# Two bias sums on GpSimd in other steps, and a prefetch hint on a loop's branch back

## The chip, the cores and the metric

The kernel runs on one core of one Trainium2 chip. The metric is the device time of the whole kernel in microseconds (us). Inputs and the weights lie in HBM. Engines are named as in the profile: PE is TensorE (PEld its weight loads), DVE is VectorE, ACT is ScalarE, POOL is GpSimd, SP is SyncE, which here only issues DMAs.

## The reference

One transformer layer on x of 16 batches x 1024 positions x 256 features, in float32: layer norm, causal attention with 16 heads of 16 features and rotary positions, beside it a feed-forward part whose output goes through a spiking neuron of five time steps, and a residual sum.

```python
xn = _layernorm(x)
x = x + attn(xn, Wq, bq, Wk, bk, Wv, bv, Wo, bo) + ffn(xn, W_fc, W_proj)

# attn
Q, K, V = (split_heads(xn @ W.T + b) for ...); Q, K = _rope(Q), _rope(K)
scores = where(causal, einsum('bhqd,bhkd->bhqk', Q, K) * 0.25, -1e9)
out = softmax(scores) @ V ; out = concat(out) @ Wo.T + bo

# ffn
h = square(relu(xn @ W_fc.T)); y = h @ W_proj.T
mem = 0.9 * mem + y - (mem > 1); spk = mem > 1      # five steps
ffn = sum(spk) / 5
```

## The kernel before

**Intervals and steps.** All five engines run programs written out by hand, tied by semaphores. A program is a row of intervals b = -1 to 15. Interval b does the attention of batch b and, beside it, the projections and the feed-forward part of batch b + 1, the layer norm of b + 2, and the output of batch b - 1. Intervals -1, 0, 14 and 15 are written out; b = 1 to 13 are one loop on each engine (`Fori(1, B - 2)`), whose closing instruction is a compare-and-branch: L1238 on PE, L683 on ACT, L960 on DVE, L589 on POOL, L485 on SP. It jumps back twelve times and falls through once. Each interval has 18 steps (n = 0 to 17), and in every step each engine does the parts that the tables at the head of the file give to that step, in the order in which its `interval` function names them. No scheduler moves anything.

**Attention.** 36 units per batch, two per step: `scores` on PE (L1156, tile pair), exp on ACT (L643, tile probs), for units on the diagonal `mask` on POOL (L556: one affine_select per 128 columns, one or two per unit), and the weighing of V by probs on PE (L1173), a step or more later by the table RUN_AT. Unit 14 stands in step 7, and its weighing in step 8. PE waits there for the mask (`mask_done`). The sums for 512 queries of four heads go out by `take_numer` on DVE (L882).

**Feed-forward.** Sixteen blocks i, by the tables EXPAND and CONTRACT: `expand` on PE (L986), relu on ACT (L634), square and high part on DVE (L846, L848), low part h_lo on POOL (L548), `contract` on PE (L1137), which waits for h_lo. Products are split in high and low parts so that three matmuls stand for one exact one. The result y is counted against thresholds on DVE (L859, L862), and the count is added to rs (L867).

**The sums of x and bias.** rs[0] and rs[1] hold 256 rows of x each, loaded by SP (L363). `add_bias` on POOL (L531 to L534) waits for the load and adds bo_sb, in two instructions of 128 x 256 (L533) per buffer, so four for both. It is called twice per batch: for the second half of the rows of batch b in step BIAS_HERE_AT, and for the first half of batch b + 1 in step BIAS_NEXT_AT. The reader is DVE's L867 (waits `rs_biased`); for the first half of b + 1 it stands in step 15, for the second half of b in step 9. SP issues the loads of the first kind in step 0 and those of the second in step 12.

**Rotary part.** Four groups u of queries and keys: PE projects (L986), DVE rotates into rot and rot_b (L769 to L776), POOL adds the two (`sum_qk`, L538, in step 3 + u), ACT squares the sum and rounds it to planes (L615, L618), DVE takes the low part (L780), SP stores both to HBM (qk_dram), and for u = 2 and 3 DVE may write rot_b only when the store of u - 2 has landed (L775).

Of the kernel before, what the change touches and what calls it, by code (L numbers as in the profile page):

```python
# [10 lines left out]
B, S, D = 16, 1024, 256  # L11
# [106 lines left out]
SPIKES_NEXT = {14 + 2 * a + part: (a, part) for a in range(2) for part in range(2)}  # L118
BIAS_HERE_AT, BIAS_NEXT_AT = 7, 14
STATS_AT = {10: range(0, 4), 11: range(4, 8)}  # L120
# [27 lines left out]
def layer_kernel(nc, x, wqk, bqk, wv, bv, wfc, wproj, wo, bo, tables, consts, selectors, out):  # L148
    edges = spike_thresholds()
    with ExitStack() as ctx:  # L150
# [157 lines left out]
        def _(sp):  # L308
# [175 lines left out]
            interval(0, True, False, True, True)  # L484
            with sp.Fori(1, B - 2) as b:  # L485
                interval(b, True, True, True, True)
# [16 lines left out]
        def _(pool):  # L503
# [26 lines left out]
            def add_bias(b, g, a):  # L530
                pool.wait_ge(rs_in[a], (b * 2 + g + 1) * 16)  # L531
                for t in range(2):
                    ins = pool.tensor_tensor(rs[a][:, t, :], rs[a][:, t, :], bo_sb[:, :], ALU.add)  # L533
                ins.then_inc(rs_biased, 1)  # L534
# [24 lines left out]
            def interval(b, att, last, more, norm, first=False):  # L559
                nb = b + 1  # L560
                for n in range(NSTEP):
                    if more and n in SUM_QK_AT:
                        sum_qk(nb, SUM_QK_AT[n])
                    if att and n == BIAS_HERE_AT:
                        for a in range(2):
                            add_bias(b, 1, a)
                    if norm and n == ROOT_AT:
# [9 lines left out]
                    if more and n in EXPAND_LATE:  # L577
                        h_low(nb, EXPAND_LATE[n])
                    if more and n == BIAS_NEXT_AT:
                        if first:  # L580
                            pool.wait_ge(bias_done, 1)
                        for a in range(2):
                            add_bias(nb, 0, a)
# [4 lines left out]
            interval(0, True, False, True, True)  # L588
            with pool.Fori(1, B - 2) as b:  # L589
                interval(b, True, True, True, True)  # L590
# [13 lines left out]
        def _(act):  # L604
# [77 lines left out]
            interval(0, True, False, True, True)  # L682
            with act.Fori(1, B - 2) as b:  # L683
                interval(b, True, True, True, True)
# [11 lines left out]
        def _(dve):  # L696
# [262 lines left out]
            interval(0, True, False, True, True)  # L959
            with dve.Fori(1, B - 2) as b:  # L960
                interval(b, True, True, True, True)
# [20 lines left out]
        def _(pe):  # L982
# [254 lines left out]
            interval(0, True, False, True, True)  # L1237
            with pe.Fori(1, B - 2) as b:  # L1238
                interval(b, True, True, True, True)
# [67 lines left out]
```

## Time and profile before

| | us |
|---|---|
| median of 3 runs | 2351.49 |
| lowest, highest | 2349.76, 2353.95 |
| the profiled execution | 2352.46 |
| its span in the trace | 2348.6 |
| PE busy | 2184.8 (93%) |
| DVE, ACT, POOL busy | 1444.0, 1435.0, 1114.9 (61%, 61%, 47%) |
| granted TensorE clock, mean | 0.976 |

The profile is of one execution. Matmuls are pipelined and their ends are modelled, so a busy PE is not one at its peak; "issue" is time in which an engine waited for nothing that the profile shows, instruction fetch among it. A wait for several semaphores is put down to the one that came last. In the timelines each row is start, duration, engine, line, operation, tiles and shapes, count, and in brackets the idle time of the engine before it, with what ended it. [...]

### The profile page before, as it was taken

To read this page: it belongs to the slowest core of one execution; us is meant where nothing else is said; L and a number is where in the kernel's file an instruction comes from. 1 tells how busy PE (TensorE), PEld (TensorE's weight loads), DVE (VectorE), ACT (ScalarE), POOL (GpSimd) and SP (SyncE) were. 2 spreads that over 40 slices of the span, in tenths; PEclk is the share of its full clock that TensorE was granted. 3 is DMA by queue.
4 is the path that set the end of the run, shared out by engine and by line. 5 is a ranking of instruction groups with operands and counts; after the bars stand their busy time and mean duration, and the time that the engine had idled before them with its cause. 6 is when DMAs were issued, how large, how long until landed. Compare 5 with 4: busy or idle time off the path is not lost.

```text
span 2348.6 us, 48369 instructions
## 1 busy us (share of the span) xinstructions
PE 2184.8 (93%) x16260; PEld 1406.9 (60%) x16260; DVE 1444.0 (61%) x2108; ACT 1435.0 (61%) x1669; POOL 1114.9 (47%) x1065
## 2 busy tenths in 40 slices
PE   3799999999999999999999999999999999999985
PEld 2656656566665656666565666656666665666632
DVE  5646575665657666665765657567565766666431
ACT  2175766657566575666667566565666657566662
POOL 2445454553545545354553545546354554545420
PEclk8999999999999999999999999999999999999987
DMA  3243453635445263453535445263443536345342
GB/s 130 96 127 102 128 165 82 185 97 141 134 111 173 80 188 95 115 174 84 172 94 158 118 110 178 80 195 96 129 147 93 175 86 177 106 124 156 93 118 57
DMA packets 167725, 297.45 MB, mean 127 GB/s; under 512 B 25008, under 2 KB 112816, under 8 KB 155056
## 3 DMA queue, kind: packets, MB, share of 16 engines
q1 hardware_dynamic: 167472, 294.01, 43.6%
q8 instruction: 167, 2.74, 0.5%
q14 instruction: 86, 0.70, 0.1%
HBM read 173.32 MB, written 102.76 MB: 118 GB/s over the span
## 4 chain that ended last, share of the span: by engine, by line
PE 75%; issue 6%; DVE 6%; ACT 6%; POOL 5%; DMA 1%; SPq 0%; DVEq 0%; ACTq 0%; POOLq 0%
PE pair L986 28%; PE pair L1173 19%; PE pair L1137 14%; PE pair L1156 13%; ACT probs L643 4%; POOL rs L533 2%; POOL probs L556 2%; DVE count L862 1%; PE pair L998 1%; DVE stats L725 1%; ACT h_sq L634 1%; POOL rot L538 1%; DMA qk_dram<-rot_b 1%; DVE h_sq L846 1%; ACT squares L615 1%
## 5 line engine op out<-in xcount | busy, mean ns | idle before, releaser
L643 ACT ACTIVATE probs<-pair 128x1024 f32<-128x1024 f32 x1152 | 1116.7, 1026 | 579.5 <-PE pair L1156 579.0
L556 POOL TENSOR_SCALAR_AFFINE_SELECT probs<-probs 128x512 f32<-128x512 f32 x512 | 403.0, 806 | 534.4 <-ACT probs L643 534.4
L1173 PE MATMUL pair<-probs,v_sb 128*17 128x512 f32 (+3 forms) x6144 | 572.0, 505 | 50.7 <-POOL probs L556 39.1
L548 POOL TENSOR_TENSOR h_lo<-h_sq,h_hi 128x512 fp32r<-128x512 f32 x256 | 386.2, 1508 | 418.0 <-DVE h_hi L848 417.6
L1156 PE MATMUL pair<-q_ring,k_ring 64*128 64x512 f32 (+3 forms) x3072 | 444.0, 382 | 40.6 <-ACT probs L643 20.2
L1156 PEld LDWEIGHTS pair<-q_ring,k_ring 64*128 64x128 f32 x3072 | 228.0, 185 | 309.0 <-ACT probs L643 164.1
L846 DVE TENSOR_TENSOR h_sq<-h_sq 128x512 f32<-128x512 f32 x256 | 189.3, 740 | 352.6 <-ACT h_sq L634 350.9
L1173 PEld LDWEIGHTS pair<-probs,v_sb 128*17 128x17 f32 x6144 | 154.7, 99 | 357.8 <-issue 268.8
L1137 PE MATMUL pair<-wproj_hi,h_hi 128*128 128x256 f32 x1024 | 293.1, 286 | 5.1 <-POOL h_lo L548 5.0
L862 DVE SCALAR_TENSOR_TENSOR count<-y_sb,count 128x512 bf16<-128x512 f32 x256 | 291.7, 1140 | 6.7
L1137 PE MATMUL pair<-wproj_lo,h_hi 128*128 128x256 f32 x1024 | 290.0, 283 | 0.0
L1137 PE MATMUL pair<-wproj_hi,h_lo 128*128 128x256 f32 x1024 | 289.8, 283 | 0.0
L634 ACT ACTIVATE h_sq<-pair 128x512 f32<-128x512 f32 x256 | 153.5, 600 | 214.1 <-PE pair L986 214.1
L538 POOL TENSOR_TENSOR rot<-rot,rot_b 128x1024 f32<-128x1024 f32 x64 | 169.2, 2644 | 217.2 <-DVE rot_b L776 217.2
L986 PE MATMUL pair<-xT_hi,wfc_hi 128*128 128x512 f32 x512 | 222.5, 435 | 5.8 <-ACT h_sq L634 3.7
L1137 PEld LDWEIGHTS pair<-wproj_hi,h_hi 128*128 128x128 f32 x1024 | 195.8, 191 | 23.8 <-issue 11.0
L986 PE MATMUL pair<-xT_hi,wfc_lo 128*128 128x512 f32 x512 | 203.0, 396 | 0.0
L986 PE MATMUL pair<-xT_lo,wfc_hi 128*128 128x512 f32 x512 | 201.1, 393 | 0.0
L1137 PEld LDWEIGHTS pair<-wproj_lo,h_hi 128*128 128x128 f32 x1024 | 196.1, 192 | 5.6
L1137 PEld LDWEIGHTS pair<-wproj_hi,h_lo 128*128 128x128 f32 x1024 | 196.2, 192 | 0.0
L882 DVE COPY numer<-pair 128x512 f32<-128x512 f32 x128 | 87.6, 685 | 120.2 <-PE pair L1173 118.6
L780 DVE TENSOR_TENSOR rot_b<-rot,planes 128x1024 fp32r<-128x1024 f32 x64 | 148.5, 2321 | 1.9 <-ACT planes L618 1.9
(87 smaller groups left out, 2598.7 us busy)
## 6 DMA issues: line engine op xcount, KB each, us to landing
q_ring<-qk_dram SPq DMA_DIRECT2D x384, 128.0 KB
k_ring<-qk_dram SPq DMA_DIRECT2D x384, 128.0 KB
qk_dram<-planes SPq DMA_DIRECT2D x64, 512.0 KB, 2.8
qk_dram<-rot_b SPq DMA_DIRECT2D x64, 512.0 KB, 3.9
xn<-in_x SPq DMA_DIRECT2D x16, 1024.0 KB, 7.1
rs<-in_x SPq DMA_DIRECT2D x64, 256.0 KB, 2.8
acc_dram<-rs SPq DMA_DIRECT2D x64, 256.0 KB, 4.4
attn<-numer SPq DMA_DIRECT2D x256, 64.0 KB, 2.3
```

What stands on the lines that cost most here:

```text
L538: pool.tensor_tensor(rot[u % 2][:, :, :], rot[u % 2][:, :, :], rot_b[u % 2][:, :, :], ALU.add).then_inc(rot_sum, 1)
L548: pool.tensor_tensor(h_lo[i % HB][:, :], h_sq[i % HB][:, :], h_hi[i % HB][:, :].bitcast(F32), ALU.subtract).then_inc(h_lo_done, 1)
L556: ins = pool.affine_select(view, view, [[0, 4], [1, P]], ALU.is_ge, 0.0, base=0, channel_multiplier=-1)
L634: act.activation(h_sq[i % HB][:, :], fc_bank, ACT.Relu).then_inc(relu_done, 1)
L643: act.activation(probs[BUFFER[n]][:, 2 * pr:2 * pr + 2, :], pair[m % NSLOT][:, :, :], ACT.Exp, scale=SCALE).then_inc(exp_done, 1)
L780: dve.tensor_tensor(rot_b[u % 2][:, :, :].bitcast(F32R), rot[u % 2][:, :, :], planes[u % 2][:, :, :].bitcast(F32), ALU.subtract).then_inc( ...
L846: dve.tensor_tensor(sq, sq, sq, ALU.mult).then_inc(sq_h, 1)
L862: dve.scalar_tensor_tensor(count[:, :], y, edges[s], count[:, :], ALU.is_gt, ALU.add).then_inc(spike_step, 1)
L986: ins = pe.matmul(bank, lhsT, rhs, start=n == 0, stop=n == len(parts) - 1)
L1137: ins = pe.matmul(proj_bank[half][:, a * D:(a + 1) * D], h[:, cols], w[:, f, :], start=f == 0 and n == 0 and a == 0, stop=f == NFT - 1 and ...
L1156: ins = pe.matmul(pair[m % NSLOT][:, half, to:to + width(kt, g)], k_ring[rows, slot, pr, kt * P:(kt + 1) * P], q_ring[rows, slot, pr, q0:( ...
L1173: ins = pe.matmul(pv_bank[32 * i:32 * i + VW, q0 - g * G:G], v_sb[:, kt, 4 * quad + i, :], probs[BUFFER[n]][:, i, at:at + width(kt, g)], s ...
```

## The change

The tables that give the steps of the two calls of `add_bias` change from 7 and 14 to 2 and 13. In POOL's `interval` the first call moves from its place ahead of the masks of its step to one behind the masks and h_lo of the step. [...]

```diff
-BIAS_HERE_AT, BIAS_NEXT_AT = 7, 14
+BIAS_HERE_AT, BIAS_NEXT_AT = 2, 13
...
-                    if att and n == BIAS_HERE_AT:
-                        for a in range(2):
-                            add_bias(b, 1, a)
                     if norm and n == ROOT_AT:
                         root(nb + 1)
...
                     if more and n in EXPAND_LATE:
                         h_low(nb, EXPAND_LATE[n])
+                    if att and n == BIAS_HERE_AT:
+                        for a in range(2):
+                            add_bias(b, 1, a)
                     if more and n == BIAS_NEXT_AT:
...
-            with pool.Fori(1, B - 2) as b:
+            with nc.Fori(1, B - 2, engines=bass.OrderedEngineSet([pool.engine]), hint_back_edge=True) as b:
                 interval(b, True, True, True, True)
```

The last edit stands in the same form for sp, act, dve and pe.

POOL's queue in interval 0, steps 0 to 9 (L556 masks, L533 the sums, L538 rotary sums, L548 h_lo), before:

```order
41 L556 AFFINE_SELECT probs<-probs 128x4x128 x8
42 L538 TENSOR_TENSOR rot<-rot,rot_b 128x1024 x2
43 L556 AFFINE_SELECT probs<-probs 128x4x128
44 L538 TENSOR_TENSOR rot<-rot,rot_b 128x1024
45 L556 AFFINE_SELECT probs<-probs 128x4x128 x4
46 L538 TENSOR_TENSOR rot<-rot,rot_b 128x1024
47 L556 AFFINE_SELECT probs<-probs 128x4x128
48 L548 TENSOR_TENSOR h_lo_57<-h_sq_49,h_hi_53 128x512
49 L533 TENSOR_TENSOR rs<-rs,bo_sb 128x256 x4
50 L556 AFFINE_SELECT probs<-probs 128x4x128 x2
51 L548 TENSOR_TENSOR h_lo_58<-h_sq_50,h_hi_54 128x512
```

and now:

```order
41 L556 AFFINE_SELECT probs<-probs 128x4x128 x8
42 L533 TENSOR_TENSOR rs<-rs,bo_sb 128x256 x4
43 L538 TENSOR_TENSOR rot<-rot,rot_b 128x1024 x2
44 L556 AFFINE_SELECT probs<-probs 128x4x128
45 L538 TENSOR_TENSOR rot<-rot,rot_b 128x1024
46 L556 AFFINE_SELECT probs<-probs 128x4x128 x4
47 L538 TENSOR_TENSOR rot<-rot,rot_b 128x1024
48 L556 AFFINE_SELECT probs<-probs 128x4x128
49 L548 TENSOR_TENSOR h_lo_57<-h_sq_49,h_hi_53 128x512
50 L556 AFFINE_SELECT probs<-probs 128x4x128 x2
51 L548 TENSOR_TENSOR h_lo_58<-h_sq_50,h_hi_54 128x512
```

The four sums stood between the first h_lo and the two mask pieces of unit 14; they stand now between the masks of step 2 and the rotary sum of u = 0.

POOL's queue in interval 0, steps 13 and 14 (with the numbers of the buffers), before:

```order
83 L548 TENSOR_TENSOR h_lo2_59<-h_sq2_51,h_hi2_55 128x512
84 L556 AFFINE_SELECT probs1<-probs1 128x4x128 x2
85 L556 AFFINE_SELECT probs2<-probs2 128x4x128 x2
86 L548 TENSOR_TENSOR h_lo3_60<-h_sq3_52,h_hi3_56 128x512
87 L548 TENSOR_TENSOR h_lo0_57<-h_sq0_49,h_hi0_53 128x512
88 L533 TENSOR_TENSOR rs0<-rs0,bo_sb 128x256 x2
89 L533 TENSOR_TENSOR rs1<-rs1,bo_sb 128x256 x2
```

and now:

```order
83 L548 TENSOR_TENSOR h_lo2_59<-h_sq2_51,h_hi2_55 128x512
84 L533 TENSOR_TENSOR rs0<-rs0,bo_sb 128x256 x2
85 L533 TENSOR_TENSOR rs1<-rs1,bo_sb 128x256 x2
86 L556 AFFINE_SELECT probs1<-probs1 128x4x128 x2
87 L556 AFFINE_SELECT probs2<-probs2 128x4x128 x2
88 L548 TENSOR_TENSOR h_lo3_60<-h_sq3_52,h_hi3_56 128x512
89 L548 TENSOR_TENSOR h_lo0_57<-h_sq0_49,h_hi0_53 128x512
```

The four sums stand now ahead of the four mask pieces of step 14 (units 28 and 29) and two h_lo, which stood ahead of them.

PE's queue at the head of the loop:

```order
 L1137 MATMUL pair<-wproj_hi,h_lo_60 128x256
 L1238 UNCONDITIONAL_BRANCH
+L1238 BRANCH_PREFETCH_HINT
 L1238 ISA
 L1151 ISA
```

One instruction came in as the first of the loop's body; nothing else on PE moved. The other engines have the same at their loop's head.

## Rows read from the trace of the kernel before

**Rows 1.** The page: busy us by engine; chain that ended last.

```profile
PE 2184.8 (93%) x16260; PEld 1406.9 (60%) x16260; DVE 1444.0 (61%) x2108; ACT 1435.0 (61%) x1669; POOL 1114.9 (47%) x1065
...
PE 75%; issue 6%; DVE 6%; ACT 6%; POOL 5%; DMA 1%; SPq 0%; DVEq 0%; ACTq 0%; POOLq 0%
PE pair L986 28%; PE pair L1173 19%; PE pair L1137 14%; PE pair L1156 13%; ACT probs L643 4%; POOL rs L533 2%; POOL probs L556 2%; DVE count L862 1%; PE pair L998 1%; DVE stats L725 1%; ACT h_sq L634 1%; POOL rot L538 1%; DMA qk_dram<-rot_b 1%; DVE h_sq L846 1%; ACT squares L615 1%
```

**Rows 2.** Waits of PE: us in total, times, longest us.

```profile
PE pair L1173 <- POOL probs L556: 39.1, 18, 2.6
...
PE pair L1156 <- issue: 18.9, 12, 1.9
...
PE pair L1173 <- issue: 4.5, 9, 0.7
```

**Rows 3.** Closing branches: count, ns min/median/max, first and last start us.

```profile
L1238 PEldq COMPARE_BRANCH  x13: 83/3404/3830, 392.4 to 2071.5; - x13
...
L960 DVEq COMPARE_BRANCH  x13: 50/56/72, 394.7 to 2073.9; - x13
```

**Rows 4.** Timeline of PE at a taken edge: start us, us, operation, [idle before].

```profile
1095.60 0.73 PE L1156 MATMUL pair<-q_ring,k_ring 64*128 64x512 f32 x4 [1.39 <-issue]
...
1098.72 0.63 PE L1173 MATMUL pair<-probs,v_sb 128*17 128x256 f32 x8 [0.55 <-issue]
```

**Rows 5.** Timeline of PE where the loop falls through.

```profile
2074.34 2.34 PE L1173 MATMUL pair<-probs,v_sb 128*17 128x512 f32 x24
```

**Rows 6.** Timeline of all engines in step 7 of the interval from 1094.

```profile
1148.22 1.95 ACT L643 ACTIVATE probs<-pair 128x1024 f32<-128x1024 f32 x2
...
1149.62 2.17 POOL L548 TENSOR_TENSOR h_lo<-h_sq,h_hi 128x512 fp32r<-128x512 f32 x1 [2.40 <-DVE h_hi L848]
...
1151.75 2.80 POOL L533 TENSOR_TENSOR rs<-rs,bo_sb 128x256 f32<-128x256 f32 x4
...
1154.51 1.91 POOL L556 TENSOR_SCALAR_AFFINE_SELECT probs<-probs 128x512 f32<-128x512 f32 x2
...
1156.47 3.48 PE L1173 MATMUL pair<-probs,v_sb 128*17 128x384 f32 x24 [2.51 <-POOL probs L556]
```

**Rows 7.** Windows (before DMA share: the granted clock), then the timeline of PE.

```profile
1156.30:1159.70 3.40, 3.23 (x24) 0.83 (x24) 2.73 (x3) 0.00 (x0) 1.52 (x2) 0.50 1.00 303
...
1437.30:1440.70 3.40, 3.37 (x32) 1.61 (x33) 2.60 (x3) 0.98 (x2) 1.40 (x1) 1.00 1.00 303
...
737.81 1.92 PE L1173 MATMUL pair<-probs,v_sb 128*17 128x384 f32 x24 [2.54 <-POOL probs L556]
```

**Rows 8.** Timeline of step 2 and 3, POOL and ACT.

```profile
704.09 2.38 POOL L538 TENSOR_TENSOR rot<-rot,rot_b 128x1024 f32<-128x1024 f32 x1 [2.34 <-DVE rot_b L776]
...
1114.75 1.23 POOL L556 TENSOR_SCALAR_AFFINE_SELECT probs<-probs 128x512 f32<-128x512 f32 x2 [1.31 <-ACT probs L643]
...
1118.52 3.31 POOL L538 TENSOR_TENSOR rot<-rot,rot_b 128x1024 f32<-128x1024 f32 x1 [2.54 <-DVE rot_b L776]
...
1121.86 1.06 ACT L615 ACTIVATE squares<-rot 128x1024 bf16<-128x1024 f32 x1 [0.41 <-POOL rot L538]
```

**Rows 9.** The sums by line: count, ns min/median/max.

```profile
L533 POOL TENSOR_TENSOR rs<-rs,bo_sb x128: 714/734/1191, 108.5 to 2252.5; 128x256 f32<-128x256 f32 x128
```

**Rows 10.** Timeline of POOL in steps 13 and 14.

```profile
1203.27 2.19 POOL L548 TENSOR_TENSOR h_lo<-h_sq,h_hi 128x512 fp32r<-128x512 f32 x1 [1.09 <-DVE h_hi L848]
...
1209.64 1.68 POOL L556 TENSOR_SCALAR_AFFINE_SELECT probs<-probs 128x512 f32<-128x512 f32 x2 [1.36 <-ACT probs L643]
```

**Rows 11.** Timeline of PE in the first and in the last interval.

```profile
114.73 0.39 PE L1137 MATMUL pair<-wproj_hi,h_hi 128*128 128x256 f32 x1 [3.05 <-POOL h_lo L548]
...
2255.88 3.32 PE L1173 MATMUL pair<-probs,v_sb 128*17 128x384 f32 x24 [1.19 <-POOL probs L556]
```

**Rows 12.** Timeline of VectorE where it waits for a store, two intervals.

```profile
713.52 0.75 DVE L775 SCALAR_TENSOR_TENSOR rot_b<-pair,neg_bqk,table 128x512 f32<-128x512 f32 x1 [3.00 <-DMA qk_dram<-rot_b]
...
1132.08 0.75 DVE L775 SCALAR_TENSOR_TENSOR rot_b<-pair,neg_bqk,table 128x512 f32<-128x512 f32 x1 [1.48 <-DMA qk_dram<-rot_b]
```

More of the change, by code:

```diff
@@ L484, in _ @@
             interval(0, True, False, True, True)
-            with sp.Fori(1, B - 2) as b:
+            with nc.Fori(1, B - 2, engines=bass.OrderedEngineSet([sp.engine]), hint_back_edge=True) as b:
                 interval(b, True, True, True, True)
@@ L682, in _ @@
             interval(0, True, False, True, True)
-            with act.Fori(1, B - 2) as b:
+            with nc.Fori(1, B - 2, engines=bass.OrderedEngineSet([act.engine]), hint_back_edge=True) as b:
                 interval(b, True, True, True, True)
@@ L959, in _ @@
             interval(0, True, False, True, True)
-            with dve.Fori(1, B - 2) as b:
+            with nc.Fori(1, B - 2, engines=bass.OrderedEngineSet([dve.engine]), hint_back_edge=True) as b:
                 interval(b, True, True, True, True)
@@ L1237, in _ @@
             interval(0, True, False, True, True)
-            with pe.Fori(1, B - 2) as b:
+            with nc.Fori(1, B - 2, engines=bass.OrderedEngineSet([pe.engine]), hint_back_edge=True) as b:
                 interval(b, True, True, True, True)
```

## The prediction

> **What bounds the kernel now.** I read the page first: which engine is busy, and which holds the chain that ended last. TensorE (PE) is busy 93% of the span and holds 75% of the chain, while VectorE, ScalarE and GpSimd (POOL) are at 61%, 61% and 47%; so an idle moment elsewhere is worth something only where PE waits for it [rows 1]. The chain by line still has 2% for the bias sums (L533), which is about 44 us of a 2348.6 us span, and 6% of "issue" [rows 1]. Next I read the list of who waited for whom, for PE alone. Three entries matter: 39.1 us in 18 waits of the weighing matmuls (L1173) for masks on POOL, 18.9 us in 12 waits of the score matmuls (L1156) for "issue", and 4.5 us in 9 waits of L1173 for "issue" [rows 2]. Twelve is the number of times the loop branches back: it runs b = 1 to 13.
>
> A steady interval is (2073.9 - 394.7) / 12 = 139.93 us, from the first and last start of VectorE's closing branch [rows 3].
>
> **Part 1, the hint.** PE's closing branch took 83 ns in its shortest case and 3404 ns at the median; VectorE's took 50 to 72 ns [rows 3]. The 83 ns is the last pass, which falls through. So a taken branch costs PE's sequencer some 3.3 us. Its queue still holds matmuls, so the array stops for less: at 1095.60 it had stood for 1.39 us, and at 1098.72 again for 0.55 us, both "issue" [rows 4]. The fall-through gives a control, the same instructions without the jump: 24 matmuls of L1173 in 2.34 us without a break [rows 5], where after the taken branch the first 16 took 1.91 us and the other 8 came 0.55 us late [rows 4].
>
> The first stop sums to 18.9 us over the 12 edges. The second sums to 7.0: 4.5 us in 9 waits, and in the other three edges it is put down to a mask, inside the 39.1 us. That share follows from the rest of the entry: the 14 waits of b = 1 to 14 at about 2.53 us are 35.4, the one of b = 15 is 1.2, and 39.1 - 35.4 - 1.2 leaves 2.5 [rows 2, 6, 7, 11]. Together **25.9 us** (2.2 per edge). SP's own hint I cost at nothing, because what it issues first after the edge (the loads of rs) is read in step 2 at the earliest. The hint instruction itself has no row; the nearest, a short branch at 50 to 83 ns [rows 3], bounds it at 13 x 0.08 = 1 us on PE if nothing covered it, and PE's queue does.
>
> [...]
>
> **Part 2, the step-7 sums leave step 7.** In the interval from 1094 POOL ends an h_lo at 1151.79, does the four sums until 1154.55, then the two mask pieces of unit 14 until 1156.42, and PE starts at 1156.47 after 2.51 us idle [rows 6]. The scores behind that mask were weighed (exp) by 1150.17 [rows 6], so nothing but the sums stands before it. Without them the mask runs at 1151.8 and takes 1.3 (rows 8 show 1.23 for two pieces) to 1.9 us: done by 1153.1 to 1153.7. PE is free at 1156.47 - 2.51 = 1153.96. The whole wait goes, in b = 1 to 14: **35.4 us**. If both bounds went the other way, 0.5 us of each would stay.
>
> With the wait goes something else. [...] The 13 windows after this wait show 0.50 in nine of the intervals and 1.00 in four; one row of each kind stands in [rows 7]. What precedes each fall is the stop of PE. Without a stop I expect no fall: 9 x 1.56 = **14.0 us**. PE's idle time is nearly nil in the rest of the interval, so I take both as kept to its end.
>
> **Part 3, where the step-2 sums land.** They stand behind the masks of step 2 and ahead of the rotary sum of u = 0 (L538). POOL is idle for 2.54 us there, from 1115.98 to 1118.52 [rows 8]. A sum takes 734 ns at the median, 714 at least and 1191 at most [rows 9]: four are 2.9 us, 4.8 at worst. So L538 starts 0.4 us late (2.3 at worst). It took 3.31 us there and 2.38 for u = 1 [rows 8]; I estimate that what slows the first passes by while it waits. ScalarE waited 0.41 us for it [rows 8], so it is on the way to the stores of the planes, for which VectorE then waits 1.48 us, and in some intervals 3.00 [rows 12]. I charge 0.3 us x 14 = **+4 us**, bounds 0 and +2.3 x 14 = +32. Behind the sums in POOL's queue stand that L538 and the masks from step 4 on. The sums wait for a load of rs that SP issues in step 0, two steps ahead, and I cost that wait at nothing.
>
> **Part 4, from step 14 to 13.** POOL ends an h_lo at 1205.46, then has two pairs of masks, the second of which its exp allows only at 1209.64; it ends at 1211.32 [rows 10]. Four sums from 1205.46 end at 1208.4 (1210.2 at worst), the first pair by 1209.7, the second, still held by its exp, by 1211.4. That is where they end today, and PE does not wait for them today. Nothing on PE: 0. VectorE no longer waits for the sums in step 15, but has slack there. In the first interval there is no attention and this VectorE wait is on the path: PE stood 3.05 us for an h_lo at 114.73 [rows 11], which VectorE squares only after it has read the sums. I take **-3 us**, once.
>
> The last interval (b = 15) has one mask wait of 1.19 us with 24 matmuls at 3.32 us [rows 11]: 1.2 + 1.4 = 2.6 at most, of which ScalarE's chain takes some: **-2 us**.
>
> Sum against this execution: -25.9 - 35.4 - 14.0 + 4 - 3 - 2 = -76.3 us. The profiled run took 2352.46 us (span 2348.6), 0.97 above the median of the three runs, 2351.49. So about 2276.2 profiled, **2275.5 us** as a median: 3.2% faster. A steady interval should be 139.93 - 2.2 - 2.5 - 9/12 x 1.56 + 0.3 = 134.4 us.
>
> **Rivals.**
> A. *The hint does nothing on PE.* The branch still takes 3.3 us. [...] Time 2275.5 + 25.9 = 2301. Chance 0.12.
> B. *Second stop stays*: the head is there at once, the block after it is not. Worth 7.0 at most: 2282. By the times in [rows 4] PE has work to cover it. Chance 0.10, inside the range.
> C. *The step-2 sums push the rotary sum by 1 us or more*, and the stores of the planes with it, so that VectorE waits and PE behind it; or the long wait of 3.00 us [rows 12], today in few intervals, comes in most (13 x 1.5 = 20 us). 2285 to 2300. For it: the chain is tight, 0.41 us. Chance 0.15.
> D. *Slower than before.* [...] Chance 0.02.
>
> **How the numbers follow.** The forecast, with B, has 0.70: its own range is 2266 (no charge in part 3, and none of the longer waits of [rows 12] left) to 2285. C has 0.15, A 0.12, D 0.02, and 0.01 is left for no change. The range from 2266 to 2300 takes in the forecast and C and stops short of A. A measurement of this kernel can tell about 0.2% (5 us) from no change; all but D and the rest lie beyond that: faster 0.97, same 0.01, slower 0.02.
>
> **What would show it.** PE's closing branch near 0.1 us at its median, and no "issue" wait of L1156 twelve times. The waits of L1173 for POOL down from 39.1 us to under 5. A granted clock of 1.00 through steps 7 and 8 of every interval. Idle time of POOL ahead of the first L538 gone, and ScalarE's wait for it still under 1 us. Steady interval 134 to 135 us. Wrong would be: the branch still at 3.3 us (A), VectorE's wait for the store of rot_b above 2 us in most intervals (C), or new "issue" stops of PE in mid-interval (D).

## The result: 3.7% faster, 3 us below the forecast range

| | before | changed kernel |
|---|---|---|
| median, us | 2350.62 (6 runs, 2347.09 to 2353.95) | 2262.97 (6 runs, 2257.88 to 2268.82) |
| ratio | 1 | 0.9627, interval 0.9609 to 0.9645 |
| profiled execution, us | 2352.46 | 2264.27 |
| its span, us | 2348.6 | 2260.7 |
| granted TensorE clock, mean | 0.976 | 0.986 |
| PE busy, us | 2184.8 | 2158.7 |
| a steady interval, us | 139.93 | 133.69 |

The forecast was 2275.5 us with a range from 2266 to 2300. The change went the way that was forecast, and PE's two kinds of stops went as described, but the time ended 12.5 us below the forecast and 3 us below the range.

The page of the changed kernel, busy time by engine and the chain that ended last, answers to [rows 1]:

```profile
PE 2158.7 (95%) x16260; PEld 1402.0 (62%) x16260; DVE 1436.7 (64%) x2108; ACT 1434.9 (63%) x1669; POOL 1091.0 (48%) x1065
...
PE 82%; DVE 6%; ACT 4%; issue 4%; POOL 2%; DMA 1%; SPq 0%; DVEq 0%; ACTq 0%; POOLq 0%
```

"POOL rs L533" is gone from the chain by line, POOL's share has fallen from 5% to 2%, and PE's has risen from 75% to 82% of a span that is 88 us shorter. PE's own busy time fell by 26 us though it does the same 16260 matmuls: the mean granted clock rose from 0.976 to 0.986, so fewer of them ran at the lower level, 0.50.

The list of PE's waits (us in total, times, longest us) answers to [rows 2]. In the answer as a whole there is no "issue" wait of L1156 or L1173 any more, and of the mask waits one is left:

```profile
PE pair L1156 <- ACT probs L643: 20.8, 33, 1.7
...
PE pair L1173 <- POOL probs L556: 0.2, 1, 0.2
```

39.1 us in 18 waits have become 0.2 us in one, and 18.9 + 4.5 us of "issue" have become nothing. The closing branches (count, ns min/median/max, first and last start), which answer to [rows 3], show the first cause:

```profile
L1238 PEldq BRANCH_PREFETCH_HINT  x13: 36/36/55, 254.8 to 1858.8; - x13
...
L1238 PEldq COMPARE_BRANCH  x13: 88/357/399, 388.3 to 1992.5; - x13
...
L960 DVEq COMPARE_BRANCH  x13: 55/61/90, 390.6 to 1994.9; - x13
```

PE's taken branch went from 3404 to 357 ns at its median. The hint instruction itself takes 36 ns. A steady interval is (1994.9 - 390.6) / 12 = 133.69 us.

The timeline of PE at a taken edge (start, us, operation) answers to [rows 4]:

```profile
1057.62 0.28 PE L1137 MATMUL pair<-wproj_hi,h_lo 128*128 128x256 f32 x1
1057.83 0.73 PE L1156 MATMUL pair<-q_ring,k_ring 64*128 64x512 f32 x4
1058.49 2.34 PE L1173 MATMUL pair<-probs,v_sb 128*17 128x512 f32 x24
1060.77 0.79 PE L1156 MATMUL pair<-q_ring,k_ring 64*128 64x384 f32 x8
```

No row has a bracket: there was no idle time. The 24 matmuls of L1173 run in one piece, in the 2.34 us of the pass that falls through [rows 5]. Both stops of [rows 4] are gone.

The timeline of step 7 in an interval of the changed kernel, POOL and PE, answers to [rows 6]:

```profile
1111.08 2.17 POOL L548 TENSOR_TENSOR h_lo<-h_sq,h_hi 128x512 fp32r<-128x512 f32 x1 [2.22 <-DVE h_hi L848]
...
1113.21 1.22 POOL L556 TENSOR_SCALAR_AFFINE_SELECT probs<-probs 128x512 f32<-128x512 f32 x2
...
1115.35 1.92 PE L1173 MATMUL pair<-probs,v_sb 128*17 128x384 f32 x24
```

The mask follows the h_lo at once, takes 1.22 us instead of 1.91, and ends at 1114.43. PE begins on it at 1115.35 with no idle time, so the mask is there 0.92 us early. The matmuls take 1.92 us instead of 3.48, because the clock stays up. The window over this place (the number before the DMA share is the granted clock) answers to [rows 7]:

```profile
1114.00:1118.00 4.00, 4.00 (x37) 1.60 (x36) 3.80 (x11) 2.69 (x4) 1.72 (x2) 1.00 0.75 182
```

PE is busy without a gap at the upper level. From b = 2 to 13 the granted clock never falls to the lower level.

### The profile page after: what moved, and what is told of

Its sections match the earlier page's. It is cut to its first block, busy times and chain, and to the rows that moved or that the text cites. A ratio compares the mean times of both kernels' runs of the same rounds, so it can differ in the third digit from the quotient of the medians.

```text
span 2260.7 us, 48434 instructions
## 1 busy us (share of the span) xinstructions
PE 2158.7 (95%) x16260; PEld 1402.0 (62%) x16260; DVE 1436.7 (64%) x2108; ACT 1434.9 (63%) x1669; POOL 1091.0 (48%) x1065
## 4 chain that ended last, share of the span: by engine, by line
PE 82%; DVE 6%; ACT 4%; issue 4%; POOL 2%; DMA 1%; SPq 0%; DVEq 0%; ACTq 0%; POOLq 0%
PE pair L986 31%; PE pair L1173 20%; PE pair L1156 15%; PE pair L1137 15%; ACT probs L643 3%; DVE count L862 2%; PE pair L998 1%; DVE stats L725 1%; POOL rot L538 1%; PE pair L1070 1%; DMA qk_dram<-rot_b 1%; ACT h_sq L634 1%; POOL probs L556 1%; DVE h_sq L846 1%; DVE denom L785 1%
## 5 line engine op out<-in xcount | busy, mean ns | idle before, releaser
L556 POOL TENSOR_SCALAR_AFFINE_SELECT probs<-probs 128x512 f32<-128x512 f32 x512 | 376.7, 756 | 507.4 <-ACT probs L643 507.4
L548 POOL TENSOR_TENSOR h_lo<-h_sq,h_hi 128x512 fp32r<-128x512 f32 x256 | 385.8, 1507 | 427.6 <-DVE h_hi L848 427.1
L1173 PE MATMUL pair<-probs,v_sb 128*17 128x512 f32 (+3 forms) x6144 | 551.4, 492 | 4.4 <-DVE numer L882 3.4
L1156 PE MATMUL pair<-q_ring,k_ring 64*128 64x512 f32 (+3 forms) x3072 | 443.1, 382 | 22.2 <-ACT probs L643 20.8
L846 DVE TENSOR_TENSOR h_sq<-h_sq 128x512 f32<-128x512 f32 x256 | 202.8, 792 | 330.9 <-ACT h_sq L634 330.8
L1156 PEld LDWEIGHTS pair<-q_ring,k_ring 64*128 64x128 f32 x3072 | 227.3, 185 | 282.8 <-ACT probs L643 183.9
L1173 PEld LDWEIGHTS pair<-probs,v_sb 128*17 128x17 f32 x6144 | 152.6, 97 | 298.9 <-issue 263.9
L862 DVE SCALAR_TENSOR_TENSOR count<-y_sb,count 128x512 bf16<-128x512 f32 x256 | 296.8, 1159 | 6.7
L538 POOL TENSOR_TENSOR rot<-rot,rot_b 128x1024 f32<-128x1024 f32 x64 | 170.2, 2659 | 172.3 <-DVE rot_b L776 172.3
```

The source lines that it names most:

```text
L538: pool.tensor_tensor(rot[u % 2][:, :, :], rot[u % 2][:, :, :], rot_b[u % 2][:, :, :], ALU.add).then_inc(rot_sum, 1)
L548: pool.tensor_tensor(h_lo[i % HB][:, :], h_sq[i % HB][:, :], h_hi[i % HB][:, :].bitcast(F32), ALU.subtract).then_inc(h_lo_done, 1)
L556: ins = pool.affine_select(view, view, [[0, 4], [1, P]], ALU.is_ge, 0.0, base=0, channel_multiplier=-1)
L846: dve.tensor_tensor(sq, sq, sq, ALU.mult).then_inc(sq_h, 1)
L862: dve.scalar_tensor_tensor(count[:, :], y, edges[s], count[:, :], ALU.is_gt, ALU.add).then_inc(spike_step, 1)
L1156: ins = pe.matmul(pair[m % NSLOT][:, half, to:to + width(kt, g)], k_ring[rows, slot, pr, kt * P:(kt + 1) * P], q_ring[rows, slot, pr, q0:( ...
```

## Where the time went: an account by stretches

Every interval has the same instructions on VectorE, so the starts of the same instruction in two traces can be subtracted. I cut each of the intervals b = 2 to 13 at three instructions of VectorE, counted from its closing branch (L960): the rotation (L770) of group u = 2, which lies about a quarter of the way in; a square (L846) some 19 us further; and a square in step 8, behind the mask wait. The table has the mean of the twelve intervals in us. "Falls" are intervals in which the granted clock drops to 0.50 behind an edge or behind step 7.

| kernel | edge and steps 0 to 3 | to step 5 | steps 6 to 8 | the rest | interval | falls |
|---|---|---|---|---|---|---|
| before | 35.73 | 18.77 | 14.12 | 71.31 | 139.93 | 9, all behind step 7 |
| changed | 33.31 | 18.71 | 10.35 | 71.31 | 133.68 | 0 |

The first column is what a taken edge costs, 2.42 us. The third is the mask wait and the clock behind it: 3.77 us, of which 2.60 is in every interval (12.95 us without a fall against 10.35) and 1.17 is the mean of the falls. The second column holds VectorE's waits for the stores of rot_b. The fourth does not move in any kernel of this study. Each kernel's account is that of one execution, the profiled one. Together 6.25 us per interval, 75 us of the 87.9 by which the span fell. The rest is in the intervals at the ends, and comes below.

## The experiments

The theory at this point: the time is PE's, in two independent places, the edge (hint) and step 7 (mask, then clock); the move from step 14 to 13 and the hints of the other engines do nothing. The rivals: the hints of the other engines matter too, the gain of the sums comes from step 13, or the steps themselves matter and not the order behind the mask.

### One part alone

Only the hints (x1):

```diff
-            with pool.Fori(1, B - 2) as b:
+            with nc.Fori(1, B - 2, engines=bass.OrderedEngineSet([pool.engine]), hint_back_edge=True) as b:
```

and the same for the other four engines.

> The kernel before with the hint on all five loops and the sums left in steps 7 and 14. My theory: the edge alone is worth the two stops of PE, 2.2 us, plus some 0.26 us that the array lost in restarting (the aligned traces of before and after show 2.42 us per edge), so 12 x 2.42 = 29 us: about 2350.6 - 29 = 2322 us. PE still waits 2.5 us for the mask of unit 14 in b = 1 to 14, and the clock still falls after it. Rival 1 (the hint and the sums need each other: a PE that is earlier only waits longer for the mask): under 10 us of gain, the waits for the mask longer than 2.5 us. Rival 2 (the hint alone explains the excess over the forecast): over 38 us.

Measured: 2312.91 us, ratio 0.9833 (0.9814 to 0.9853) to a before of 2353.15. That is 40 us, more than the edges alone can give, 12 x 2.42 = 29, and 9 us below the 2322 that I had expected. The account shows 33.31, 18.68, 13.18, 71.32, interval 136.49. The first column is exactly that of the changed kernel. The third has come down by 0.94 us though the sums are still ahead of the mask: the falls went from nine to two. Two windows behind step 7 of this kernel, one of an interval with a fall and one without:

```profile
588.70:592.10 3.40, 2.79 (x24) 0.83 (x24) 3.16 (x4) 0.00 (x0) 1.96 (x2) 0.50 1.01 319
725.00:729.00 4.00, 2.26 (x28) 0.88 (x28) 3.90 (x5) 1.02 (x2) 3.10 (x3) 1.00 0.94 311
```

Ahead of both, PE had stood for the same 2.52 us. So a stop of this length is followed by a fall at some times and not at others. How often goes with PE's hint: of twelve intervals, nine, eight and eight have a fall behind step 7 in the three kernels with the sums ahead of the mask and no hint on PE (before, x4, x6), and two in each of the two with it (x1, x3).

Only the sums, both in their new steps (x2):

```diff
-BIAS_HERE_AT, BIAS_NEXT_AT = 7, 14
+BIAS_HERE_AT, BIAS_NEXT_AT = 2, 13
...
-                    if att and n == BIAS_HERE_AT:
-                        for a in range(2):
-                            add_bias(b, 1, a)
...
+                    if att and n == BIAS_HERE_AT:
+                        for a in range(2):
+                            add_bias(b, 1, a)
```

> The changed kernel without the hint. My theory: the mask waits (2.6 us in b = 1 to 14: 36 us), nine falls of the clock (1.47 us each: 13 us), the last interval (6 us) and fewer late stores (0 to 4 us) go, the edges stay with their 3.3 us branches: 55 to 59 us of gain, about 2293 us. If the two halves do not add up (rival), this run plus the one with the hint alone differ from 88 us together by more than 8 us.

Measured: 2294.69 us, 0.9763 (0.9739 to 0.9786). Account: 35.79, 18.92, 10.35, 71.30, interval 136.37. The first column is that of before and the third that of the changed kernel. PE's waits keep the "issue" entries; of the mask's 39.1 us, 1.7 us in two waits are left, both behind an edge:

```profile
PE pair L1156 <- issue: 19.3, 12, 1.9
...
PE pair L1173 <- issue: 4.3, 9, 0.7
```

The two gains multiply to 0.9833 x 0.9763 = 0.960, against 0.9627 for both: 98.7 us one by one, 87.7 together. What each change alone takes away with the clock (most of the falls in x1, all of those behind step 7 in x2) can be had only once.

### Whose hint it is

The hint on PE alone (x3), and on the four others without PE (x4):

```diff
-            with pe.Fori(1, B - 2) as b:
+            with nc.Fori(1, B - 2, engines=bass.OrderedEngineSet([pe.engine]), hint_back_edge=True) as b:
```

> The kernel before with the hint on PE's loop alone. My theory: the whole gain of the hint is PE's, so the same time as with all five hints, about 2322 us within 4 us, and SP still has 2.8 us from its branch to its next instruction. Rival: part of the gain comes from SP issuing the next interval's DMAs 2.8 us sooner; then this run is slower than the one with all hints by over 6 us.

> The kernel before with the hint on the four other engines, not on PE. My theory: no change, within 4 us of 2350.6; PE's branch stays at 3.3 us and more, SP's next instruction comes 0.2 us after its branch instead of 2.8. Rival (SP's delay matters): 6 us or more faster.

Measured: x3 2312.06 us, 0.9824 (0.9798 to 0.985), the same as all five hints. x4 2355.42 us over ten runs, 1.0007 (0.9994 to 1.002), the same as before. One of PE's waits and its closing branch in x4:

```profile
PE pair L1156 <- issue: 18.3, 12, 1.7
...
L1238 PEldq COMPARE_BRANCH  x13: 83/3409/3607, 394.2 to 2076.9; - x13
```

The other engines' hints do change something that can be counted: the instruction fetches by the DMA queues of the page (packets, MB, share), here of before and then of the changed kernel.

```profile
q8 instruction: 167, 2.74, 0.5%
q14 instruction: 86, 0.70, 0.1%
```

```profile
q8 instruction: 156, 2.56, 0.5%
q14 instruction: 28, 0.23, 0.0%
```

In x4 q8 stays at 167 and q14 falls to 28, in x3 q8 falls to 156 and q14 stays at 87. So q8's drop belongs to PE's hint, q14's to the others', and 58 fetches fewer on q14 are worth nothing in time. The whole gain of the hint is PE's. As for x1, the time of x3 lies below the 2322 us expected, and for the same reason, the falls: two in its loop.

### Which of the two moves of the sums

Only the step from 14 to 13 (x6):

```diff
-BIAS_HERE_AT, BIAS_NEXT_AT = 7, 14
+BIAS_HERE_AT, BIAS_NEXT_AT = 7, 13
```

> The kernel before with the second call of the sums in step 13 instead of 14, and nothing else. My theory: nothing in the loop, since PE waited for neither; at most 0.5 us in the first interval, where the changed kernel gained 0.4 us instead of the 3 that I had forecast. So 2352 us within 4. Rival (the first interval's wait for h_lo was due to the sums in step 14 alone): 3 us less there, and PE's wait of 3.05 us near 114 us gone without others in its place.

Measured: 2350.32 us over ten runs, 1.0002 (0.9985 to 1.0018) to a before of 2347.72. Account: 139.93 before, 140.04 here. In the loop it is worth nothing, and in the whole time nothing beyond the 4 us that the interval leaves open. In the first interval the trace does show a gain, of 1.9 us; it is told below, under part 4.

The changed kernel with this move undone (x10: BIAS_NEXT_AT = 14, all else as changed):

```diff
-BIAS_HERE_AT, BIAS_NEXT_AT = 7, 14
+BIAS_HERE_AT, BIAS_NEXT_AT = 2, 14
```

> The changed kernel with the second call of the sums left in step 14. My theory: that call is worth nothing in either place once PE is not waiting, so 2263 us within 4 and a steady interval of 133.5 to 134.1 us. Rival: step 14 delays the mask of unit 31, which PE now reads sooner than before (its mask ended at 1220.50 where the weighing began at 1220.84): a wait of PE for POOL once per interval, and over 3 us in all.

Measured: 2263.03 us, 0.9619 (0.9603 to 0.9635). The changed kernel has 0.9627. Same.

### The step, or the place behind the mask

The sums stay in step 7 and only go behind the masks and the h_lo of that step; no hint (x7):

```diff
-                    if att and n == BIAS_HERE_AT:
-                        for a in range(2):
-                            add_bias(b, 1, a)
...
+                    if att and n == BIAS_HERE_AT:
+                        for a in range(2):
+                            add_bias(b, 1, a)
```

> The kernel before with the sums still in step 7, but behind the masks and the h_lo of that step, and no hint. My theory: what counts is that the sums stand ahead of the mask of unit 14, not how early they are; so the part from step 7 to the middle of step 8 takes 10.35 us in place of 12.95 to 14.6, as with the sums in step 2, and the time is that of the sums-only kernel, 2295 us within 5. Rival (they must be early, since behind the mask they delay the h_lo of step 8 and the reader on VectorE in step 9): new waits of PE for POOL or a stretch to the end of the interval above 71.3 us; over 2305 us.

Measured: 2300.42 us, 0.9794 (0.9767 to 0.982). Account: 36.34, 18.66, 10.35, 71.30, interval 136.66. The third column is the full gain of the changed kernel, and no delay appears behind the sums. The timeline of POOL in its step 7:

```profile
448.00 2.18 POOL L548 TENSOR_TENSOR h_lo<-h_sq,h_hi 128x512 fp32r<-128x512 f32 x1 [2.21 <-DVE h_hi L848]
450.14 1.22 POOL L556 TENSOR_SCALAR_AFFINE_SELECT probs<-probs 128x512 f32<-128x512 f32 x2
...
454.99 4.36 POOL L533 TENSOR_TENSOR rs<-rs,bo_sb 128x256 f32<-128x256 f32 x4
459.31 1.28 POOL L548 TENSOR_TENSOR h_lo<-h_sq,h_hi 128x512 fp32r<-128x512 f32 x1
```

The sums take 4.36 us there, longer than ahead of the mask (2.80 in [rows 6]), and the next h_lo starts behind them without idle time, and yet PE waits for none of it. The ratio is 0.003 above that of x2, some 7 us; the two intervals of the ratios overlap, so the times alone do not tell them apart. In the account 0.55 us per interval, 6.6 us in all, stand in the first column. In six of the twelve intervals the clock falls behind the edge; in the kernel before it never did. The six have 36.9 us in the first column, the other six 35.8: a fall there costs 1.05 us net, and the six together 6.3 of the 6.6 us. It is less than the 1.6 us by which the matmuls take longer, since PE's second stop (3.0 us in six waits of this run) comes only in the six intervals without a fall behind the first. Here is one, PE's timeline and the window over it:

```profile
392.58 0.73 PE L1156 MATMUL pair<-q_ring,k_ring 64*128 64x512 f32 x4 [1.74 <-issue]
393.24 3.96 PE L1173 MATMUL pair<-probs,v_sb 128*17 128x512 f32 x24
```

```profile
393.50:397.50 4.00, 4.00 (x28) 1.00 (x22) 0.25 (x1) 1.55 (x2) 0.64 (x1) 0.57 0.42 133
```

The 24 matmuls that take 2.34 us in [rows 5] take 3.96 at the lower clock. That the falls and not the place of the sums made the difference to x2 (which has one such fall) can be tried from one side: take the stop at the edge away with the hint, and a price of the place itself would be left. So x12 is x7 with the hints and with BIAS_NEXT_AT = 13:

```diff
-BIAS_HERE_AT, BIAS_NEXT_AT = 7, 14
+BIAS_HERE_AT, BIAS_NEXT_AT = 7, 13
```

> The changed kernel with the first call of the sums in step 7, behind the masks and h_lo of that step, where without the hint it took away PE's wait as well as step 2 did. My theory: the same as the changed kernel, 2263 us within 4, stretch of steps 7 and 8 at 10.35 us, and the 1.3 us by which that kernel's edges were dearer than those of the sums-only one (37 us to the second rotation, with falls of the clock at the edge) do not come with the hint. Rival: the place in step 7 itself costs some 5 us more in all, through the h_lo of step 8.

Measured: 2265.26 us, 0.9628 (0.9606 to 0.965), the same as the changed kernel. Account: 33.33, 18.65, 10.35, 71.31, interval 133.64, no falls in the loop. No such price is left, so step 2 is no better a place than step 7 behind the mask. Why x7 has six falls at the edge and x2 one is not shown. What counts is that nothing long stands between the h_lo of step 7 and its mask.

### How much delay the mask can take

Two of the four sums ahead of the mask, two behind (x8, no hint):

```diff
                     if att and n == BIAS_HERE_AT:
-                        for a in range(2):
-                            add_bias(b, 1, a)
+                        add_bias(b, 1, 0)
...
+                    if att and n == BIAS_HERE_AT:
+                        add_bias(b, 1, 1)
```

> The kernel before with one buffer's two sums ahead of the mask of unit 14 in step 7 and the other two behind it, no hint. It is a half dose of the wait. My theory: PE's wait shrinks by the 1.4 us of two sums, from 2.5 to 1.1 us, and after a stop this short the granted clock does not fall (it did not after the 1.4 us stops at the edges): 1.4 + 0.75 x 1.47 = 2.5 us per interval, 14 times, and part of the last interval: about 2314 us. Rival (the clock falls after any wait there): the falls stay in most intervals and the time is about 2330 us. Second rival (PE's wait is not for the sums but for exp): no change in the wait.

Measured: 2307.85 us, 0.9821 (0.9796 to 0.9846). Account: 36.01, 18.88, 10.89, 71.31, interval 137.08. PE's mask waits in the list, and the place in one interval (the added line moves the numbers of PE's lines by one):

```profile
PE pair L1174 <- POOL probs L556: 7.4, 15, 0.8
```

```profile
450.33 1.43 POOL L533 TENSOR_TENSOR rs<-rs,bo_sb 128x256 f32<-128x256 f32 x2
451.73 1.21 POOL L556 TENSOR_SCALAR_AFFINE_SELECT probs<-probs 128x512 f32<-128x512 f32 x2
```

```profile
453.00 1.92 PE L1174 MATMUL pair<-probs,v_sb 128*17 128x384 f32 x24 [0.48 <-POOL probs L556]
```

I had expected 1.1 us of wait and got 0.5. It follows from the 0.92 us by which the mask is early without sums: the two sums hold it for 451.73 - 450.33 = 1.40 us, and 1.40 - 0.92 = 0.48. The same sum for the kernel before, from [rows 6]: the four sums hold it for 1154.51 - 1151.75 = 2.76, the two mask pieces take 1.91 instead of 1.21, and 2.76 + 0.70 - 0.92 = 2.54, where the row has 2.51. Behind the 0.48 us the clock never fell: the matmuls take 1.92 us. (Three falls stand behind edges, as in x7.)

### How late the rotary sum may come

The forecast charged 0.3 us per interval for L538 starting later. The place in the changed kernel and, second, in x1, where no sums stand there (timelines of POOL and ScalarE):

```profile
543.52 2.83 POOL L533 TENSOR_TENSOR rs<-rs,bo_sb 128x256 f32<-128x256 f32 x4
...
546.30 3.38 POOL L538 TENSOR_TENSOR rot<-rot,rot_b 128x1024 f32<-128x1024 f32 x1
...
549.72 1.06 ACT L615 ACTIVATE squares<-rot 128x1024 bf16<-128x1024 f32 x1 [0.69 <-POOL rot L538]
```

```profile
554.71 1.06 ACT L615 ACTIVATE squares<-rot 128x1024 bf16<-128x1024 f32 x1 [0.41 <-POOL rot L538]
...
557.70 1.94 ACT L643 ACTIVATE probs<-pair 128x1024 f32<-128x1024 f32 x2 [0.98 <-PE pair L1156]
```

L538 comes 0.28 us later (0.69 against 0.41). Behind it ScalarE has 0.98 us in which it only waits for PE, and the delay goes in there. To find where that slack ends I made the sums longer without more work on data: each in four pieces of 128 x 64 (x9), and in eight of 128 x 32 (x11), for the step-2 sums only, all else as in the changed kernel:

```diff
+                w = D // 4 if g else D
...
-                    ins = pool.tensor_tensor(rs[a][:, t, :], rs[a][:, t, :], bo_sb[:, :], ALU.add)
+                    for c in range(0, D, w):
+                        ins = pool.tensor_tensor(rs[a][:, t, c:c + w], rs[a][:, t, c:c + w], bo_sb[:, c:c + w], ALU.add)
```

> The changed kernel with each sum of step 2 cut in four pieces of 64 columns, so that the same work takes POOL longer (estimate from 734 ns for 256 columns and 200 ns for 8: 16 x 0.32 = 5.1 us in place of 2.9); the rotary sum of u = 0 then starts some 2.6 us late. It doses the term that I had charged with 0.3 us per interval. My theory now: ScalarE waits for the rotary sum, and VectorE for the store of its planes: the stretch around it grows by 1 to 2.5 us, 14 to 33 us in all, 2277 to 2296 us. Rival (the path has slack of 3 us and more): no change from 2263 us within 4.

> The changed kernel with each sum of step 2 cut in eight pieces of 32 columns, a second dose after the four pieces (which took POOL 5.5 us in place of 2.8 and cost 0.9 us per interval in the loop). From 327 ns for 64 columns and 200 ns for 8 I estimate 32 x 0.25 = 8 us or somewhat more. My theory: ScalarE has 0.98 us of slack behind its wait for the rotary sum, and beyond that the delay goes through one to one: L538 ends 4.5 to 5.5 us late against the kernel before, so 3.5 to 4.5 us per interval less what the DMA wait of VectorE gives back (1.5): 2 to 4 us, 28 to 56 us in all, 2291 to 2320. Rival (the cost of the first dose was the many small instructions and not the delay): under 10 us above 2263 plus 12.

Measured: x9 2287.43 us, 0.973 (0.9705 to 0.9756); x11 2315.74 us, 0.9858 (0.9832 to 0.9884). In the account x9 has 33.97, 18.93, 10.36, 71.31, interval 134.57, and x11 36.58, 18.86, 10.37, 71.31, interval 137.12. In both the lines stand two further down. First x9, then x11:

```profile
548.29 5.51 POOL L535 TENSOR_TENSOR rs<-rs,bo_sb 128x64 f32<-128x64 f32 x16
...
556.17 1.06 ACT L617 ACTIVATE squares<-rot 128x1024 bf16<-128x1024 f32 x1 [2.38 <-POOL rot L540]
...
558.08 3.75 ACT L645 ACTIVATE probs<-pair 128x1024 f32<-128x1024 f32 x4
```

```profile
551.40 7.88 POOL L535 TENSOR_TENSOR rs<-rs,bo_sb 128x32 f32<-128x32 f32 x32
...
561.63 1.06 ACT L617 ACTIVATE squares<-rot 128x1024 bf16<-128x1024 f32 x1 [4.73 <-POOL rot L540]
...
564.60 0.50 PE L1158 MATMUL pair<-q_ring,k_ring 64*128 64x512 f32 x2 [2.26 <-ACT probs L645]
```

With 5.51 us of sums ScalarE stands 2.38 us, its slack is used up (its exps then run four in a row without a pause), and an interval costs 0.9 us. With 7.88 us ScalarE stands 4.73 us, PE's next scores wait 2.26 us for an exp, and the interval costs 3.4. The slack of 0.98 us read in x1 orders all three. The delay of L538 is 0.28 us in the changed kernel, 2.38 - 0.41 = 1.97 in x9 and 4.73 - 0.41 = 4.32 in x11; less 0.98 that is nothing, 0.99 and 3.34, and the intervals cost 0, 0.9 and 3.4 more. (In x11 three intervals also have a fall of the clock behind PE's new stops, 0.3 us of the 3.4.)

So rival C's delay begins to cost where the forecast put it, at a delay of 1 us, and the change stays well below. But the path is another than C's. C had VectorE wait longer for the stores of rot_b. Three lines of the waits (us in total, times, longest us), of x9 and then of x11, tell which waits grew:

```profile
DVE rot_b L777 <- DMA qk_dram<-rot_b: 68.1, 31, 2.9
...
PE pair L1158 <- ACT probs L645: 31.8, 50, 4.5
...
DVE rot_b L782 <- ACT planes L620: 18.5, 16, 5.2
```

```profile
PE pair L1158 <- ACT probs L645: 61.1, 65, 3.4
...
DVE rot_b L777 <- DMA qk_dram<-rot_b: 52.0, 30, 2.9
...
DVE rot_b L782 <- ACT planes L620: 48.1, 16, 3.5
```

In the changed kernel the three are 71.6, 20.8 and 1.9 us. The wait for the stores shrinks; VectorE waits for ScalarE's planes instead, and PE for its exps.

The profiled execution of x9 is 28.8 us longer in its span than that of the changed kernel (its median 24). The loop has 12 x 0.89 = 10.7 of them, the stretch up to the end of b = 1 another 4.1, b = 14 and b = 15 have 7.0 each. In b = 14 GpSimd stopped in the middle of the 16 pieces, for nothing that the profile shows:

```profile
2035.13 3.94 POOL L535 TENSOR_TENSOR rs<-rs,bo_sb 128x64 f32<-128x64 f32 x14 [5.47 <-issue]
```

PE then stood 4.53 us for an exp at 2044.46. This stop is in no other trace of this study at that place, and its cause is not shown. The 7 us of b = 15 belong to a spread that the next section describes.

## Which steps of the prediction held, and which failed

Both mechanisms were forecast rightly: PE's stops at the edge, and the mask wait with the clock behind it, give 74.2 of the 87.9 us. The size was not, and the measured time lies below the range. Two steps failed. The first is a mechanism: part 3 took the step-2 sums to be on a path that PE waits for and charged +4 us; the runs show no charge, and with the stores the term came out 4.3 us better than forecast. The second is a size: the low end of the range, 2266, moved that one charge to zero (and took away long stores), and left no room for the other terms to come out larger. The last interval gave 6.2 us where 2 were forecast, the edges 29.0 where 26.4 were, b = 1 4.7 where 2.2 were. Part of that is luck: the last interval and b = 1 vary from trace to trace without the edit ordering them. (A slip of 0.3 us is in the sum as well: 2276.2 less 0.97 is 2275.2, not 2275.5.)

**Part 1, the hint: right in kind, 2.6 us short.** Forecast 25.9 us, 2.16 per edge; measured 2.42 per edge in the account, in x1, x3 and the changed kernel alike (35.73 to 33.31). The term was made of PE's idle time. Of the 0.26 left out, 0.20 can be read as overlap that a stop breaks off: in [rows 4] the 16 matmuls, the break and the 8 behind it take 1.91 + 0.55 + 0.63 = 3.09 us, and the 24 in one piece 2.34 [rows 5], so a gap of 0.55 us cost 0.75. I had the control at hand ([rows 5]) and used it to find the second stop, not to size it. The branch was put near 0.1 us and took 0.357; PE's queue covered it. Rival A fell, and so did rival B: the second stop went with the first. In the trace of the changed kernel neither a stop at the head nor one behind it is left, and x1, with the hints alone, has no "issue" wait of L1156 or L1173 either.

**Part 2, the mask: right.** Forecast 2.53 us per interval; measured 2.60, or 0.8 us more over the loop (1.2 in the table below, which goes by the forecast's rounded 2.5). Where it goes was right: the mask straight behind the h_lo, finished before PE is free.

**Part 2, the clock: right in size, with a wider cause than I saw.** Nine falls of 1.56 us (3.48 - 1.92, the 24 matmuls at a granted clock of 0.50 and at 1.00 [rows 6, 7]) were forecast to go, and the account has 1.17 us per interval, which is 9 / 12 x 1.56. x1 shows that the same stop of 2.6 us is followed by a fall in two intervals of twelve rather than nine, and x7 shows falls behind the edge stops of 1.8 us (21.6 us in 12) in six of twelve. No fall in the loop of any of these kernels came without a stop ahead of it. Whether one comes behind a given stop is not settled by its length, and what settles it stays open. So the nine falls that went with the mask wait were no fixed sum: seven of them go with the hint alone as well.

**Part 3, step 2: the step that failed.** Charge +4 us, bounds 0 and +32; measured 0: the first column of the account is 33.31 with the sums in step 2 (changed kernel) and 33.31 and 33.33 with them in step 7 (x1, x12). The step that failed is the inference "ScalarE waits 0.41 us for L538, so it is on the way to the stores". I read the wait ahead of L615 and not the next one: 0.98 us of idle time behind it. A delay has to use up every wait further down before it counts. The estimate that L538 would be quicker when it starts later failed too: 3.38 us against 3.31 in [rows 8]. The waits for the stores of rot_b [rows 12], which rival C made more of, hardly moved: 74.2 us in 32 waits before, 71.6 in 32 now, and 2.3 of the 2.6 us between them are one wait in b = 1. In b = 2 to 13 two waits for the store of u = 0 of 3.0 and 3.3 us are gone, and four of 2.0 to 2.2 us have come. Over the loop the second column fell by 0.06 us and I had it rise by 0.3: 4.3 us.

**Part 4, step 13: right in the loop, 1.9 of the 3 us in the first interval.** x6 and x10 confirm the 0 in the loop. In the first interval PE's wait of 3.05 us for an h_lo [rows 11] has been cut up. The timeline of PE there in the changed kernel:

```profile
115.85 0.39 PE L1137 MATMUL pair<-wproj_hi,h_hi 128*128 128x256 f32 x1 [0.80 <-POOL h_lo L548]
...
120.82 0.39 PE L1137 MATMUL pair<-wproj_hi,h_hi 128*128 128x256 f32 x1 [1.89 <-POOL h_lo L548]
```

A third of 1.03 us follows. What the move gave has to be read around the sums alone. From a cast of VectorE ahead of them (L848, at 97.16 us before and 99.57 in the changed kernel) to a row of xn behind them (L744, at 124.21 and 124.76) it is 27.05 us before and 25.19 in the changed kernel: 1.86 us gained. The five others with the sums in step 13 (x2, x6, x9, x11, x12) have 25.18 to 25.20 us there, and of those with step 14 four have 27.05 to 27.07 (x1, x3, x4, x8) and two 26.50 and 26.51 (x10, x7; why these two differ is not shown). The gain is hidden in the changed kernel's start, because the stretch ahead of that cast took 2.4 us longer in this execution. Measured against before, that stretch is between 1.0 us shorter and 2.4 us longer in the traces of this study, and the edits do not order it.

**The last interval: short by 4 us, and that by chance.** For b = 15 I had -2 us. It took 107.7 us of the span before and 101.3 in the changed kernel. But the windows over that interval (the number before the DMA share is the granted clock) in, first, the kernel before, then the changed kernel, x2 and x9 show what it follows:

```profile
2207.40:2315.10 107.70, 90.58 (x683) 40.24 (x682) 25.13 (x32) 70.69 (x77) 27.36 (x37) 0.87 0.38 98
```

```profile
2125.70:2227.00 101.30, 84.86 (x683) 38.85 (x681) 23.33 (x32) 70.45 (x77) 25.29 (x36) 0.93 0.41 104
```

```profile
2154.60:2253.80 99.20, 82.97 (x683) 39.29 (x682) 23.34 (x32) 70.46 (x77) 25.63 (x37) 0.95 0.42 106
```

```profile
2147.40:2255.70 108.30, 92.59 (x684) 40.63 (x682) 23.39 (x32) 70.62 (x77) 27.37 (x49) 0.86 0.39 97
```

In b = 15 nothing stands beside the attention, so PE has many short idle times (in the kernel before 25, 0.7 us on average and 1.2 at most), and the clock goes up and down. The length goes with the mean clock: 99.2 at 0.95, 101.3 at 0.93, 107.7 at 0.87, 108.3 at 0.86. x1, with the mask wait of b = 15 left as it was, has 100.7 us; x10, without it, 106.9. x1 and x3 have the same program on PE and the same median within 1 us, and b = 15 is 7 us longer in x3's trace. The edit does not order them. So some 4 us of the 12 were not to be had from the profile; it belongs in a range, as the spread of one stretch whose clock is not steady.

The whole difference, spans: 87.9 us measured against 76.3.

| where | forecast | measured | more by |
|---|---|---|---|
| loop, 12 edges | 26.4 | 29.0 | 2.6 |
| loop, mask and clock | 44.0 | 45.2 | 1.2 |
| loop, step 2 and stores | -3.6 | 0.7 | 4.3 |
| b = 1 | 2.2 | 4.7 | 2.5 |
| b = 14 | 2.2 | 2.7 | 0.5 |
| b = 15 and the end | 2 | 6.2 | 4.2 |
| start | 3 | -0.7 | -3.7 |

(The forecast's loop goes by its own rounded 2.2 + 2.5 + 1.17 - 0.3 per interval.) In b = 1 the extra is a late store: VectorE waited 3.80 us for it before and 1.49 in the changed kernel, 3.34 in x1, 1.51 in x2 and 3.38 in x12, so this too is chance. What the low end of the range left out were the upper sides of these terms: 0.26 per edge, a last interval whose clock can be worth 6 us, and a late store. **Rival D**, slower than before, shows nowhere: the hints took 40 us off in x1 and cost nothing in x4 (1.0007), there is no new "issue" wait of PE in mid-interval, and the fetches on q8 fell from 167 to 156.

## What to carry to other kernels

When a loop's body is long, look at the closing branch of the engine that sets the time, compare its taken time with the fall-through, and look for a second "issue" stop a few microseconds on; here a hint on that one engine was enough. A side job on a helper engine goes behind what the bounding engine waits for in that step, and it need not move to another step; its room is the time by which the waited-for result is early (0.92 us here), and the price of a delay is what is left after every idle time further down the chain has been used (0.98 us here). Where a stop of TensorE goes, count what the clock did behind it too, but keep it apart from the wait: it is not there in every interval, and it can be removed only once. A range gets room for each term on both sides, not only for the one that is in doubt.

## What the runs showed of the hardware

- A taken branch on PE took 3404 ns without and 357 ns with the hint (medians), and the hint itself 36 ns (39 on VectorE). On VectorE the taken branch takes 50 to 72 ns without a hint, and its hint and those of ScalarE, GpSimd and SyncE change no time (x4, ratio 1.0007) though they take q14's fetches from 86 to 28.
- The lower clock after a stop of PE is not a matter of the stop's length alone. Behind 2.5 to 2.6 us it came in 9 of 12 intervals in one kernel and in 2 of 12 in another; behind 1.4 to 2.0 us at the edge in none, none, one, three and six of 12 (before, x6, x2, x8, x7); behind 0.5 us in none. In these five kernels every fall at the edge came behind a stop of 1.7 us or more, but in x6 seven such stops had none. The 24 matmuls behind a stop took 3.26 or 3.48 us instead of 1.92, or 3.96 instead of 2.34; in the interval's length a fall cost 1.3 to 1.7 us behind step 7 and about 1.1 at the edge in x7.
- GpSimd's sum depends little on its size when small: 734 ns for 128 x 256 in [rows 9], 327 ns for 128 x 64 (median of x9), 256 ns for 128 x 32 (x11). Four times the pieces made 2.83 us into 5.51, eight times into 7.88. The same four sums took 2.80 us ahead of the mask and 4.36 behind it in the same step; what made them slower there was not tried.
